# An early high part from its own PSUM bank in a recurrence of 1024 steps

## What is computed

```python
layer = base_layer + einsum('bdr,bkr->bdk', x_a, x_b)      # from cond, per sequence
y = x + (x + einsum('btc,bco->bto', x, layer))             # first layer with its residual
def step(prev_h, xw):
    next_h = tanh(prev_h @ Wh + xw)                        # xw = y @ Wx + b
    return (next_h, next_h)
_, h_t = scan(step, h0=cond, xW_t)                         # 1024 steps, one after the other
out = y + h_t
```

## Time and profile before

| what | value |
|---|---|
| three runs | 850.0, 848.36, 849.58 us; median 849.58 |
| span of the profiled execution (first to last instruction) | 847.7 us |
| median of the runs less this span | 1.9 us |
| PE busy | 679.0 us (80%), 15861 matmuls |
| PE loading weights | 589.7 us (70%) |
| DVE busy, ACT busy | 259.5 us (31%), 258.4 us (30%) |
| granted TensorE clock | 1.000 |
| DMA | 9.63 MB, 11 GB/s in the mean |

### The profile page before, as it was taken

One profiled execution on the slowest core, in us unless ns is written; L12 is line 12 of the kernel. 1 busy time (PEld: TensorE's weight loads), 2 busy tenths in 40 slices (PEclk: granted clock), 3 DMA queues, 4 the chain that ended last, 5 costly groups with the idle time before them and its releaser, 6 DMA issues.

```text
span 847.7 us, 36688 instructions
## 1 busy us (share of the span) xinstructions
PE 679.0 (80%) x15861; PEld 589.7 (70%) x15861; DVE 259.5 (31%) x1411; ACT 258.4 (30%) x2069; POOL 6.2 (1%) x17
## 2 busy tenths in 40 slices
PE   5688788888788888787888787888787888787885
PEld 5577676777676777676777676777676777676774
DVE  6433223233222233222233232233232233232232
ACT  6232332332332232233233233223223323323322
POOL 2000000000000000000000000000000000000000
DMA  7000000000000000000000000000000000000000
GB/s 252 5 9 5 6 6 2 6 6 5 6 6 3 5 6 5 6 6 4 4 6 5 6 6 4 3 6 5 6 6 5 3 6 5 6 6 5 3 3 5
DMA packets 12091, 9.63 MB, mean 11 GB/s; under 512 B 1813, under 2 KB 11056, under 8 KB 12080
## 3 DMA queue, kind: packets, MB, share of 16 engines
q1 hardware_dynamic: 11984, 9.45, 3.7%
q0 software_dynamic: 96, 0.02, 0.0%
HBM read 7.36 MB, written 2.10 MB: 11 GB/s over the span
## 4 chain that ended last, share of the span: by engine, by line
PE 80%; ACT 12%; issue 5%; DMA 1%; SPq 1%; DVE 1%; DVEq 0%; another core or an unknown queue 0%
PE acc L302 40%; PE acc L307 19%; ACT h_hi L422 12%; PE acc L287 8%; PE p_y L271 7%; PE acc L283 2%; PE p_o L266 2%; DMA x_in<-x_dram 1%; PE p_x L261 1%; SPq L207 1%; PE p_y L380 0%; SPq L204 0%; DVE lay_s L630 0%; DVE lay_f L626 0%; PE acc L394 0%
## 5 line engine op out<-in xcount | busy, mean ns | idle before, releaser
L302 PE MATMUL acc<-h_hi,wh_s 128*128 128x2 f16 x8192 | 381.1, 168 | 150.4 <-ACT h_hi L422 148.5
L302 PEld LDWEIGHTS acc<-h_hi,wh_s 128*128 128x128 f16 x8192 | 300.1, 106 | 232.7 <-ACT h_hi L422 219.2
L422 ACT ACTIVATE h_hi<-acc 128x4 f16<-128x4 f32 x1023 | 177.0, 173 | 572.7 <-PE acc L307 572.7
L512 DVE TENSOR_TENSOR h_lo<-h_f,h_hi 128x4 f16<-128x4 f32 x1024 | 167.2, 163 | 567.3 <-ACT h_f L424 567.1
L307 PE MATMUL acc<-h_lo,wh_s 128*128 128x2 f16 x4096 | 271.5, 170 | 0.0
L307 PEld LDWEIGHTS acc<-h_lo,wh_s 128*128 128x128 f16 x4096 | 188.4, 107 | 0.0
L424 ACT ACTIVATE h_f<-acc 128x4 f32<-128x4 f32 x1024 | 172.2, 168 | 0.6 <-PE acc L307 0.6
L287 PE MATMUL acc<-y_s,wx_s 128*128 128x16 f16 x2048 | 94.6, 176 | 0.0
L271 PE MATMUL p_y<-x_s,lay_s 128*128 128x32 f16 x1024 | 75.0, 239 | 2.2 <-DVE lay_s L630 2.2
L287 PEld LDWEIGHTS acc<-y_s,wx_s 128*128 128x128 f16 x2048 | 73.9, 104 | 2.9
L271 PEld LDWEIGHTS p_y<-x_s,lay_s 128*128 128x128 f16 x1024 | 57.7, 125 | 2.7 <-DVE lay_s L630 2.7
(11 more groups left out here) (68 smaller groups left out, 93.2 us busy)
## 6 DMA issues: line engine op xcount, KB each, us to landing
w_f<-w_dram SPq DMA_DIRECT2D x8, 512.0 KB, 9.4
x_in<-x_dram SPq DMA_DIRECT2D x32, 64.0 KB, 2.3
out_dram<-o_row SPq DMA_DIRECT2D x64, 32.0 KB, 1.9
w_f<-w_dram SPq DMA_DIRECT2D x1, 256.0 KB, 3.0
base_f<-base_dram SPq DMA_DIRECT2D x1, 256.0 KB, 11.2
wh_f<-wh_dram SPq DMA_DIRECT2D x1, 256.0 KB, 10.7
wx_f<-wx_dram SPq DMA_DIRECT2D x1, 256.0 KB, 10.7
cond_r<-cond_dram SPq DMA_DIRECT2D x1, 2.0 KB
```

What stands on the lines that cost most here:

```text
L302: nc.tensor.matmul(dst[:, mo * NB:(mo + 1) * NB], wh_s[:, pw, ki, mo * P:(mo + 1) * P], h_hi[:, par, ki, :], start=False, stop=True, skip_ ...
L422: nc.scalar.activation(h_hi[:, par].rearrange("p m b -> p (m b)"), src, func, scale=scale).then_inc(s_hhi[half], 1)
L512: nc.vector.tensor_sub(h_lo[:, par].rearrange("p m b -> p (m b)"), h_f[:, slot, :], h_hi[:, par].rearrange("p m b -> p (m b)")).then_inc(s ...
```

## The change

The state gets a high part that is made before the sum is complete. A fifth and a sixth PSUM bank (`pre`, one for each half) hold, for each step, the input part a second time. Onto it PE adds only the four products of the high weights with `h_rnd`, the float16-rounded exact state. From that near-sum ACT takes `h_pre` (float16), the new high part. The full sum still gets eight products with `h_pre` and four with `h_lo`, where `h_lo` is now the exact state less `h_pre`. So a step has sixteen products: the eight of `h_pre` in one run, then the four of `h_rnd` onto the early bank, then the four of `h_lo`. ACT does three tanh per step (`h_pre`; then `h_f` and `h_rnd`, with `h_f` first), where it did two.

```diff
-            def chain_step(half, u):
+            def chain_step(half, u, last=False):
...
+                pe.wait_ge(s_hpre[half], u + 1)
+                for mo, ki in TILES:
+                    onto(full, 1, mo, ki, h_pre)
+                for mo, ki in TILES:
+                    onto(full, 0, mo, ki, h_pre)
+                if not last:
+                    pe.wait_ge(s_hrnd[half], u + 1)
+                    for mo, ki in TILES:
+                        done = onto(early, 0, mo, ki, h_rnd)
+                    done.then_inc(s_presum[half], 1)
                 pe.wait_ge(s_hlo[half], u + 1)
+                for mo, ki in TILES:
+                    done = onto(full, 0, mo, ki, h_lo)
+                done.then_inc(s_sum[half], 1)
...
             def half_block(half, last=False):
                 for u in range(HALF):
+                    final = last and u == HALF - 1
+                    n = half * HALF + u + 1
+                    if not final:
+                        act.wait_ge(s_presum[half], u + 1)
+                        give_pre(n, pre[half][:, u * COLS:(u + 1) * COLS], ACT.Tanh, 1.0 / SCALE)
                     act.wait_ge(s_sum[half], u + 1)
+                    give_h(n, acc[half][u % 2][:, (u // 2) * COLS:(u // 2 + 1) * COLS], ACT.Tanh, 1.0 / SCALE,
+                           rounded=not (last and u >= HALF - 2))
+                act.sem_clear(s_presum[half])
                 act.sem_clear(s_sum[half])
...
-        PAUSES = 4
+        PRE = 2
+        INPUT = [(slot, *product) for slot in (0, PRE, 1) for product in PRODUCTS]
+        BEFORE = 2 * len(PRODUCTS)
...
+                    if slot == PRE:
+                        dst, n, t = pre[half], HALF, slice(half * HALF, (half + 1) * HALF)
```

The input part of a half grows from 36 to 54 products: the 18 for the early bank cover all 16 steps in one go (32 columns each, where the others have 16). The side work is dealt out anew, by step u of a half (the list of 54 is the even bank, the early bank, the odd bank, each beginning with its two bias products):

```diff
 half A:
-  u = 2..5: nine of the 36 input products of half B
+  u = 2..9: seven of the 54 input products of half B
+  u = 10: turn_x;  u = 13, 14, 15: four of the first layer's 32 products (EARLY, 12)
 half B:
-  u = 0: turn_x;  u = 4..7: eight of the first layer's 32 products
-  u = 12..15: nine of the 36 input products of half A
+  u = 0, 2, 3, 4: five of the first layer's products (LATE, 20)
+  u = 9..15: eight of the 54 input products of half A
```

More of the change, by code:

```diff
@@ L107, in cond_recurrence @@
         h_f = sb("h_f", [P, BLOCK, COLS])
-        h_hi = sb("h_hi", [P, 2, NM, NB], F16)
+        h_pre = sb("h_pre", [P, 2, NM, NB], F16)
+        h_rnd = sb("h_rnd", [P, 2, NM, NB], F16)
         h_lo = sb("h_lo", [P, 2, NM, NB], F16)
@@ L114, in cond_recurrence @@
         acc = [[pb(f"acc{half}{par}", [P, 512]) for par in range(2)] for half in range(2)]
-        p_x = pb("p_x", [P, 512])
+        pre = [pb(f"pre{half}", [P, 512]) for half in range(2)]
+        p_xo = pb("p_xo", [P, 512])
         p_y = pb("p_y", [P, 512])
-        p_o = pb("p_o", [P, 512])
-        p_ab = pb("p_ab", [P, 4 * P], F16)
         s_cond, s_vec, s_w1, s_b2, s_base = sem("s_cond"), sem("s_vec"), sem("s_w1"), sem("s_b2"), sem("s_base")
@@ L288, in input_products, with share @@
                                          start=False, stop=True, skip_group_check=True)
-            def share(todo, k):
-                n = len(todo) // PAUSES
+            def share(todo, n, k):
                 return todo[k * n:(k + 1) * n]
-            def chain_step(half, u):
+            EARLY, LATE = LAYER[:12], LAYER[12:]
+            def chain_step(half, u, last=False):
                 par = u % 2
[L297 to L303, removed]
-                pe.wait_ge(s_hlo[half], u + 1)
[L305 to L309, removed]
@@ L311, in half_a, with onto @@
-            def half_a(first=False):
+                full = acc[half][par][:, (u // 2) * COLS:(u // 2 + 1) * COLS].rearrange("p (m b) -> p m b", b=NB)
+                early = pre[half][:, u * COLS:(u + 1) * COLS].rearrange("p (m b) -> p m b", b=NB)
+                def onto(dst, pw, mo, ki, h):
+                    return nc.tensor.matmul(dst[:, mo, :], wh_s[:, pw, ki, mo * P:(mo + 1) * P], h[:, par, ki, :],
+                                            start=False, stop=True, skip_group_check=True)
@@ L328, in half_b @@
                 for u in range(HALF):
-                    chain_step(B, u)
+                    chain_step(B, u, last=last and u == HALF - 1)
                     if u == 1:
@@ L440, in _ @@
                 for dst in (hid_s[:, m, 0, :], hid[:, m, :]):
-                    last = nc.scalar.activation(dst, p_o[:, m * NB:(m + 1) * NB], ACT.Gelu, bias=vec_c[:, 2, m:m + 1])
+                    last = nc.scalar.activation(dst, p_xo[:, 256 + m * NB:256 + (m + 1) * NB], ACT.Gelu, bias=vec_c[:, 2, m:m + 1])
             last.then_inc(s_hidhi, 1)
@@ L460, in _ @@
             act.wait_ge(s_condc, 1)
+            give_pre(0, cond_c[:, :], ACT.Copy, 1.0)
             give_h(0, cond_c[:, :], ACT.Copy, 1.0)
@@ L512, in chain_step, with half_a @@
                 nc.vector.tensor_sub(h_lo[:, par].rearrange("p m b -> p (m b)"), h_f[:, slot, :],
-                                     h_hi[:, par].rearrange("p m b -> p (m b)")).then_inc(s_hlo[half], 1)
-            def half_a(first=False):
+                                     h_pre[:, par].rearrange("p m b -> p (m b)")).then_inc(s_hlo[half], 1)
+            def half_a(first=False, last=False):
                 for u in range(HALF):
                     chain_step(A, u)
-                    if first:
-                        continue
[L520 to L525, removed]
+                    if not first:
+                        if u == 0:
+                            sum_out(B)
+                        if u == 2:
+                            keep_y()
+                        if u == 3:
+                            row_out()
+                    if last:
+                        continue
+                    if u == 11:
+                        split_x_high()
+                    if u == 12:
+                        split_x_low()
                 dve.sem_clear(s_hf[A])
@@ L637, in _ @@
             half_a(first=True)
-            with dve.Fori(0, NBLOCK - 1):
+            with dve.Fori(0, NBLOCK - 2):
                 half_b()
                 half_a()
+            half_b()
+            half_a(last=True)
             half_b(last=True)
```

122 lines of the change are left out of this document (67 added, 55 removed).

## The result

The changed kernel takes **825.84 us** (median of four runs, 825.67 to 826.21) where the one before takes 849.49 beside it: a ratio of 0.972, with a 95% interval of 0.9707 to 0.9734. The forecast was 824.4, within 808 to 846. The profiled execution spans 824.1 us (847.7 before); 822.5 was predicted.

The account below looks back on a forecast made before the run. The prediction took the early loop to bound the changed kernel; -46.3 + 12.8 + 7.3 + 1.0 = -25.2 us against the 847.7 span gave 822.5, plus 1.9 between span and median: 824.4 us, range 808 to 846.

Parts of the forecast that it names:

- The early loop: h_rnd products to h_pre's tanh 0.28, to first h_pre product 0.23, eight products 0.24: 0.748 us, setting the step's period.
- The gain of the bare steps: Steps shortened from 0.7933 to 0.748 us, 1022 times: 46.3 us less.
- The exact loop: Loop through h_lo products, h_f and h_rnd or the subtraction: alone needs 0.72 us, so does not bound; DVE slack 0.04.
- Bias products: Pauses around 3-row products on PE, hidden before, now exposed: steps of 0.803 or 0.829 us, +12.8 us in all.
- The early bank's products: Input products with 32 columns in adjacent pairs, taken 0.027 us apart; upper bound 0.050 would add 11.6 us.
- The loop's end: PE's step over the back edge, with a third semaphore clear at 0.12 us: 1.02 us, +7.3 us in all.
- Ahead of the recurrence: Before the first steps: 18 more input products, a copy from float32, the first step's 18 side products: +1.0 us.
- the bias pauses or the loop's end are hidden (2): Rival: pauses around 3-row products shrink when PE is full, or clears run ahead: 804 to 812 us; chance 0.08.
- Cover too thin (3): Rival: wide products at 0.050, ACT order or a transpose's tail cost time: 836, 842 or 847 us; chance 0.12.
- No gain in the step (4): Rival: the third wait in PE's stream costs 0.045, what the early sum gives: 849 to 850 us; chance 0.03.
- The code stream (1): Rival: PE's longer loop body no longer stays, each back edge waits 1.5 to 2.3 us: 869 to 893; chance 0.10.

## Why the prediction was right

**The early loop** (0.28 + 0.23 + 0.24, carried as 0.748) measured 0.7467. The gain of the bare steps was 1022 x 0.0466 = 47.6 us, 46.3 predicted. The mechanism was right; that the period was met to 0.001 is in part luck, since the prediction itself allowed 0.01 for the rounding of the rows, 10 us in all. The two runs with products behind and the one with the tanh order turned show that this isn't a coincidence of sums: each loop moves the period by what it is made of.

**The exact loop** with slack of 0.04 to 0.06 was right: over the subtraction, turned into the bound, it runs at its old 0.79, and over h_rnd at 0.733 and 0.760 with one and two products more in it.

**Bias products** were predicted at 0.803 and 0.829 a step, +12.8 us. At the head of a share they take just that, 0.800 and 0.827. In the middle they take 0.820 and 0.847: 0.02 more. The prediction had priced all three like the one at the head. The 0.02 is what the neighbours in the middle last longer: an input product with 16 or 32 columns lasts 0.176 or 0.189 against 0.165 for an h_lo product, and a bias product with 32 columns 0.192 against 0.180. That the pause is counted from a product's end fits these numbers and was not tested. The term was 15.1 us: 0.2 a half A, 0.28 a half B.

**The early bank's products**, taken at 0.027, measured 0.027; the upper bound of 0.050 and its 11.6 us didn't occur. The Trainium skill (PSUM — Partial Sum Buffer, Specifications) says that any non-contiguous pattern slows matmuls significantly. Here the products that write pairs of adjacent columns, with starts 16 bytes apart, are not slowed; the layer's, which write single columns 16 bytes apart, stand 0.050 apart. The layer's products also read x by single columns where the input's read y by pairs, so these runs don't tell whether the writing or the reading costs it.

**The loop's end** was predicted at 1.02, +7.3 us; it took 1.04 at the 29 back edges taken and 0.89 where the loop ends, +7.9 in all. The run with the clears moved shows that two of the three clears were 0.24 of the 0.29.

**Ahead of the recurrence**, 1.0 predicted: the span is 824.1, and 847.7 - 47.6 + 15.1 + 7.9 = 823.1 leaves 1.0 for it and for the end. The rows bear it out: the first tanh that waits for a product starts at 32.17 against 31.39, and the next comes 1.10 behind it against 0.99.

So the sum was 1.6 us low: the bare steps gave 1.3 more, the bias products cost 2.3 more and the loop's end 0.6 more. Part of the error cancelled.

**The rivals.** That the bias pauses or the loop's end are hidden (2) is refuted by the steps themselves. Cover too thin (3): neither wide products nor ACT's order nor a transpose cost anything. No gain in the step (4): a wait that is met in time costs nothing; the h_rnd and h_lo products follow at 0.027 spacing. The code stream (1) did not stall, with 16 packets, but it was priced too low: a back edge whose code isn't on the chip costs 4.9 us beyond one whose code is, and not 1.5 to 2.3. Had the body been too long, the kernel would have taken some 29 x 4.9 = 142 us more, 968, if a body of one block cost as much to fetch again as one of two, which no run shows. What failed there is the premise that one packet's time is the price: some 12 packets come in each round, and PE stops twice. The Trainium skill (Runtime: NRT & Kernel Launch, Instruction fetch mechanics) gives PE 2048 instructions, and the runs agree: 1320 stay, 2640 don't. The Trainium skill's window of two pages there, outside of which a taken branch has to fetch, they don't bear out: 30 rounds of the loop came with 16 packets in all.

## What to carry to other kernels

In a chain of short steps, write down every loop that closes on itself, with the starts of its instructions from the timeline, and compare their sums: the longest is the period, and the next longest tells how much can be gained before it takes over. An engine whose share of work grows by a third can still carry a shorter period, if the added work stands beside the loops; but then its pauses, hidden before, are paid in full, so look at each pause (a change of row count, a clear, a branch) that the old period covered, and deal the side work out in portions that fit the new cover.

## What the runs showed of the hardware

- A pair of 3-row products between 128-row ones costs 0.19 to 0.21 us beyond its two spacings. The same products padded with zero rows cost the plain 0.027 each.
- A clear on PE takes 0.12 us of its sequencer's time, twice what its own row says (0.056). Moved ahead of waits in the last step of a half, two of them left the path (1.04 to 0.80 us).
- Four products of one run lasted 0.24 when their wait was met 0.06 early, 0.26 when it was met at their turn and 0.27 when it was met 0.05 late: a release that is not early costs more than its lateness.
- A taken back edge takes 0.21 us in its own row. To code that is no longer on the chip it costs about 4.9 us more, in two stops (3.6 us in the branch itself, the other in the step after next), with some 12 packets.
